# Graph attention over 200,000 sorted edges: tiles gathered once, block crossings through three extra one-hot slots, and the loads of a round in four transfers

## The reference

```python
h = (x @ W).reshape(N, H, C)
alpha = leaky_relu(a_src[src] + a_dst[dst], 0.2)      # per edge and head
m = segment_max(alpha, dst)
e = exp(alpha - m[dst])
denom = segment_sum(e, dst)
out = segment_sum((e / denom[dst])[:, :, None] * h[src], dst)
```

## Time and profile before

| what | value |
|---|---|
| median of 3 runs | 7430.2 us (7429.2 to 7434.15) |
| the profiled execution | 7443.6 us, its span 7441.7 us |
| PE, DVE, POOL busy | 69%, 68%, 71% of the span |
| three edge phases | about 2107, 2108 and 2286 us |
| four node phases | about 207, 181, 343 and 207 us |

### The profile page before, as it was taken

The page is one execution under the profiler, slowest core; times in us unless marked ns, Lnnn a source line. Parts: engine busy times, 40 slices in busy tenths (PEclk is TensorE's granted clock), DMA queues, the critical chain, the costliest instruction groups (busy, mean ns, idle before and its releaser), DMA issues. The chain is left out here.

```text
span 7441.7 us, 104504 instructions
## 1 busy us (share of the span) xinstructions
PE 5099.7 (69%) x22377; PEld 3596.7 (48%) x22378; DVE 5094.2 (68%) x15120; ACT 1891.8 (25%) x3056; POOL 5272.6 (71%) x5626
## 2 busy tenths in 40 slices
PE   7577777777777677777777776867667667676660
PEld 5354554555445445554555444554445445444440
DVE  4666666666667766666666666976666666666669
ACT  4222222222223422222222221222222222222214
POOL 1677777777774677777777775867777677777657
PEclk8677777777777877777777777987777777877775
DMA  8444444444444544444444443555444444444434
GB/s 180 128 139 137 137 137 139 138 137 136 138 138 114 163 137 137 136 139 138 137 136 138 138 137 105 172 161 140 131 136 131 134 133 132 134 132 135 129 95 133
DMA packets 559563, 1017.17 MB, mean 137 GB/s; under 512 B 203404, under 2 KB 356705, under 8 KB 558884
## 3 DMA queue, kind: packets, MB, share of 16 engines
q0 software_dynamic: 242256, 675.99, 33.8%
q1 hardware_dynamic: 246114, 270.22, 12.5%
q10 hardware_dynamic: 70514, 65.01, 2.8%
HBM read 941.47 MB, written 69.28 MB: 136 GB/s over the span
## 5 line engine op out<-in xcount | busy, mean ns | idle before, releaser
L908 POOL DMA_INDIRECT e_rows<-table,e_idx x4992 | 4770.3, 956 | 1724.0 <-issue 1434.4
L979 PE MATMUL e_p_mm<-e_rows,e_onehot 128*128 128x264 f32 x9984 | 3242.9, 480 | 390.0 <-DVE e_rows L1073 388.1
L979 PEld LDWEIGHTS e_p_mm<-e_rows,e_onehot 128*128 128x128 f32 x9984 | 2232.5, 235 | 1013.4 <-issue 590.0
L1073 DVE TENSOR_TENSOR e_rows<-e_rows,e_p_e 128x1024 f32<-128x1024 f32 x1248 | 1504.8, 1206 | 0.0
L942 ACT ACTIVATE e_onehotT<-e_onehotT,minus_pidx 128x2048 bf16<-128x2048 bf16 x312 | 624.5, 2002 | 1506.3 <-DMA e_passb<-pass_rows 1506.3
L1065 DVE TENSOR_TENSOR e_onehot<-e_col,e_p_iota 128x512 f32<-128x512 bf16 x1248 | 836.2, 670 | 108.7 <-issue 105.9
L1126 DVE TENSOR_TENSOR e_srcm<-e_p_one,e_mask 64x128 f32<-64x128 f32 (+1 forms) x312 | 89.2, 286 | 1174.5 <-PE e_p_one L1007 951.3
L975 PE MATMUL e_p_mm<-zeros 1*128 1x264 bf16 x1248 | 322.3, 408 | 643.6 <-DVE e_rows L1073 643.6
L958 ACT ACTIVATE e_rows<-e_gap 128x64 f32<-128x64 f32 (+1 forms) x312 | 85.5, 274 | 2562.3 <-DVE e_gap L1196 2562.3
L945 ACT ACTIVATE e_onehotT<-e_onehotT,one_col 128x2048 bf16<-128x2048 bf16 x312 | 624.6, 2002 | 10.3
L1164 DVE SCALAR_TENSOR_TENSOR e_top<-e_mask,e_p_small,e_seg 64x128 f32<-64x128 bf16 (+1 forms) x312 | 110.3, 353 | 742.7 <-PE e_p_small L1025 742.7
(11 more groups left out here) (214 smaller groups left out, 5536.0 us busy)
## 6 DMA issues: line engine op xcount, KB each, us to landing
e_onehotT<-rel_rows SPq DMA_DIRECT2D x312, 512.0 KB
e_rows<-table,e_idx POOLq DMA_INDIRECT x4992
table<-n_row ACTq DMA_DIRECT2D x196, 130.0 KB, 2.9
n_looprow<-table SPq DMA_DIRECT2D x196, 128.0 KB, 2.4
e_mask<-mask_rows SPq DMA_DIRECT2D x208, 80.0 KB
e_mask<-mask_rows SPq DMA_DIRECT2D x104, 160.0 KB
table<-n_row ACTq DMA_DIRECT2D x98, 132.0 KB, 1.8
n_node<-in_x_pad SPq DMA_DIRECT2D x98, 128.0 KB, 3.6
```

The lines of the kernel that those rows point to most:

```text
L908: pool.indirect_dma_start(rows[k][:, g, 0:TW], None, table[L], bass.IndirectOffsetOnAxis(ap=idx[k][:, g:g + 1], axis=0)).then_inc(s_gat[k] ...
L979: ins = nc.tensor.matmul(p_mm[:, bass.ds(region, MW)], onehot[:, g, :], rows[k][:, g, :], start=False, stop=True, skip_group_check=True)
L1073: return nc.vector.tensor_tensor(feats, feats, p_e[:, g4, :].unsqueeze(3).to_broadcast([P, 4, H, C]), ALU.mult)
```

## The change

A tile is gathered once. `TILES` is rounded up to 1568, so a layer has 98 windows. A tile belongs to the block of its first edge. Where a tile of the window reaches into a next block, one of three extra slots (`EXTRAS`) holds a second one-hot of it, relative to that block; the slots are worked through in every window, needed or not. DVE makes their one-hots and copies of the tile's messages at the start of the body (`extras`), PE multiplies them after the zeros (`extras`) and looks up three more scores into a zeroed `p_look`. Edges outside of a slot's block match nothing, so the validity mask and its addition (`srcm`) are gone, and DVE scans straight from PSUM. Windows that span four blocks or more take a new branch (`far_blocks`, on PE and DVE) that loops over all 98 blocks; the word `slow` is gone, and PE reads a flag and the words of the slots behind the first transpose. SP issues four transfers: indices and columns as one float32 row block of 67 columns (`loaded`), `onehotT` with 19 slots instead of 16, `mask` with 4 rows instead of 5, and all passes together. ACT copies the columns out of `loaded` (51 columns) behind `srcc`, and its two passes over `onehotT` are 2432 columns wide. `ACC_W` goes from 272 to 264. The tables are made in another way (`tile_tables` for `step_tables`), without the repeated gather of edges.

```diff
-                    wait_apart(sp, st["compact"], ago(BUFS))
-                    sp.dma_start(idx[k][:], src_dram[bass.ds(w, 1), :, :].rearrange("w p g -> p (w g)")
-                                 ).then_inc(s_idx[k], 16)
+                    wait_apart(sp, st["cols"], ago(BUFS))
+                    sp.dma_start(loaded[k][:], col_dram[:, bass.ds(w * COL_W, COL_W)]).then_inc(s_idx[k], 16)
...
+                    wait(act, st["settled"], ago(BUFS))
+                    nc.scalar.copy(col[k][:], loaded[k][:, 0:AT_SRC]).then_inc(st["cols"], 1)
...
+                def extras():
+                    for e in range(EXTRAS):
+                        r = (1 + e) * BANK
+                        nc.tensor.matmul(p_mm[:, r:r + MW], onehot[:, G + e, :], xmsg[:, e, :], start=False, stop=True,
+                                         skip_group_check=True)
...
                     if not first:
-                        regions = words(pe, 0, (w - 1) * G, G)
-                        slow, = words(pe, 3, (w - 1) * WIN + REGIONS, 1)
+                        regions = words(pe, REGION_ROW, (w - 1) * G, G, (REGIONS - 1) * BANK)
...
-                    offs = words(pe, 1, w * G, G)
+                    offs = words(pe, AD_ROW, w * G, G, (BLOCKS - 1) * ADS_W)
+                    flag, *extra_ad = words(pe, WINDOW_ROW, w * WIN + W_FLAG, 1 + EXTRAS, (BLOCKS - 1) * ADS_W)
+                    slots = words(pe, WINDOW_ROW, w * WIN + W_TILE, EXTRAS, G - 1)
...
+                    nc.tensor.matmul(p_look, zeros[:, 0:P], zeros[:, 0:3 * HG], start=True, stop=False, skip_group_check=True)
                     for g in range(G):
-                        last = nc.tensor.matmul(p_look[:, g * 3 * H:(g + 1) * 3 * H], onehotT[k][:, g * P:(g + 1) * P],
-                                                ad_parts[:, bass.ds(offs[g], 3 * H)], start=True, stop=True)
+                        lookup(k, g, slice(g * 3 * H, (g + 1) * 3 * H), offs[g])
+                    far_blocks(None if first else (k - 1) % BUFS, k, flag, far_count(pe, w), past)
+                    for e in range(EXTRAS):
+                        last = lookup(k, G + e, bass.ds(slots[e] * (3 * H), 3 * H), extra_ad[e])
                     last.then_inc(st["lookup"], 1)
-                    if not first:
-                        late_products((k - 1) % BUFS, slow, past)
...
+                def extras(k, slots, done, before):
+                    wait(dve, s_mm[0], before)
+                    one_hot(G, EXTRAS, k, G, p_iota[:, 0:P])
+                    dve.wait_ge(st["expo"], done)
+                    if TOPS:
+                        dve.wait_ge(st["topread"], done)
+                    flat_rows = rows[k][:].rearrange("p g m -> p (g m)")
+                    for e, slot in enumerate(slots):
+                        feats = flat_rows[:, bass.ds(slot * MW, D)].rearrange("p (h c) -> p h c", h=H)
+                        weight = p_e_flat[:, bass.ds(slot * H, H)].unsqueeze(2).to_broadcast([P, H, C])
+                        nc.vector.tensor_tensor(xmsg[:, e, 0:D].rearrange("p (h c) -> p h c", h=H), feats, weight, ALU.mult)
+                        last = nc.vector.tensor_copy(xmsg[:, e, D:MW], flat_rows[:, bass.ds(slot * MW + D, MW - D)])
+                    last.then_inc(st["extras"], 1)
...
                     if not first:
-                        off, _, _, _, slow = words(dve, 3, (w - 1) * WIN, REGIONS + 1)
+                        off, = words(dve, WINDOW_ROW, (w - 1) * WIN, 1, (BLOCKS - 1) * ACC_W)
+                        slots = words(dve, WINDOW_ROW, (w - 1) * WIN + W_TILE, EXTRAS, G - 1)
                         if not second:
-                            offs = words(dve, 3, (w - 2) * WIN, REGIONS)
+                            offs = words(dve, WINDOW_ROW, (w - 2) * WIN, REGIONS, (BLOCKS - 1) * ACC_W)
+                    flag, = words(dve, WINDOW_ROW, w * WIN + W_FLAG, 1, 2)
...
+                    if not first:
+                        extras((k - 1) % BUFS, slots, past, ago(2))
                     dve.wait_ge(s_ld[k], turns * N_LOAD)
                     dve.wait_ge(st["srcT"], now)
-                    nc.vector.tensor_tensor(srcm[:], p_src[0:HG, 0:P], m[0:HG, 0, :], ALU.add).then_inc(st["masked"], 1)
-                    dve.wait_ge(st["masked"], now)
-                    nc.vector.tensor_tensor_scan(fwd[:], m[0:HG, 1, :], srcm[:], -BIG, ALU.add, ALU.max)
+                    nc.vector.tensor_tensor_scan(fwd[:], m[0:HG, 0, :], p_src[0:HG, 0:P], -BIG, ALU.add, ALU.max)
```

More of the change, by code:

```diff
@@ L186, in on_pool @@
-            pool.wait_ge(s_p0off, 48)
-            pool.dma_start(off_row[0:3, :], off_dram[:]).then_inc(s_p0o, 16)
-            with nc.allow_non_contiguous_dma(reason="a few words per window, once"):
-                by_group = win_dram[:].rearrange("(j w) c -> w j c", w=P // G)
-                pool.dma_start(by_group[:, :, 0:REGIONS], win_i[0:P:G, :, 0:REGIONS]).then_inc(s_p0win, 16)
-                pool.dma_start(by_group[:, :, REGIONS:WIN], win_i[G - 1:P:G, :, REGIONS:WIN]).then_inc(s_p0win, 16)
@@ L192, in on_pool @@
[L192 to L202 removed]
+            nc.gpsimd.memset(zero_row[:], 0.0)
@@ L303, in step_tables @@
-        return start, on_pool, on_dve, first_blocks, columns
+            nc.vector.tensor_single_scalar(own[:], own[:], 7, ALU.logical_shift_right)
+            nc.vector.tensor_scalar(masks4[:, :, 0, :], first, -BIG, None, ALU.mult)
+            link(nc.vector.tensor_scalar(masks4[:, :, 1, :], last, -BIG, None, ALU.mult))
+            link(nc.vector.tensor_tensor(own_f[:, 1, :], own[:, 0, :], own[:, 1, :], ALU.subtract))
+            link(nc.vector.tensor_scalar(own_f[:, 1, :], own_f[:, 1, :], float(REGIONS), -FAR, ALU.is_ge, ALU.mult))
@@ L982, in product, with lookup @@
                         ins.then_inc(s_mm[g // 4], 1)
[L984 to L992 removed]
+                def lookup(k, slot, column, ad):
+                    return nc.tensor.matmul(p_look[:, column], onehotT[k][:, slot * P:(slot + 1) * P],
+                                            ad_parts[:, bass.ds(ad, 3 * H)], start=False, stop=True, skip_group_check=True)
```

563 lines of the change are left out of this document (320 added, 243 removed).

## The result

The changed kernel takes 7324.3 us (median of 4 runs, 7302.9 to 7338.8), the kernel before 7431.1 (4 runs, 7429.2 to 7434.2): ratio 0.985, 95% interval 0.982 to 0.989. On another chip it was 7314.1 against 7457.9 (0.981, 0.979 to 0.983). The forecast was slower, 7480: the sign was wrong. The time misses the forecast's own range of 7400 to 7560 and lies in the wide one, 7190 to 7690, which took in its rivals. The profiled execution took 7302.9 us, the lowest of the four.

What follows compares the result with a forecast made beforehand. POOL's gathers bound the first two edge phases, the PE-DVE ring the third; afterwards the ring everywhere. Phase terms +46 and +11, node phase -8, gave +49 on 7430.2, rounded 7480 us; own range 7400 to 7560, wide 7190 to 7690.

Steps and rivals of the forecast that it cites:

- (d): DVE's work for the extra slots: hidden in ordinary windows, +1.55 us at the loop's turn, every third window.
- half of the stall in the third phase: DVE's issue stall before L1126, third edge phase: 1.0 us per window today, 0.5 kept because moved code might keep it.
- 20.6 + 1.9: Third edge phase, us per window: ring without the stall plus the three new products, 22.5; half the stall makes 23.0.
- the gains: Savings per window on the ring: -0.31 us for srcm and its wait, -0.86 for PE's load of slow with register work.
- The ring through PE and DVE: Cycle of PE and DVE waits per window: about 19.7 us before, 21.6 mean after, above POOL's 20.15 in all phases.
- second rival: The change works as meant: ring below POOL's pace, -371 - 8, so 7051 us; chance 0.1.
- first rival: DVE's loop turn gets cheap as its body shortens: all windows ordinary at 20.8 us, third phase -116, 7194 us; chance 0.2.
- (a): Three extra-slot products on PE ahead of products(0) delay DVE's top: +1.9 us per window, bounds +1.5 and +2.9.
- gain of 1.6 for products(0): If more matmuls kept PE's full clock: products(0) 1.6 us shorter per window, with the three new products at +1.5.
- (b): PE's added register words, zero matmul and three lookups, mostly hidden in its wait ahead of the zeros: +0.25 us, bounds 0 and 0.6.
- The first node phase: Start of the kernel, before the first edge phase: new tables ready earlier, -8 us, or 0 if they aren't.
- slow rival: Fetch of DVE's code stalls the loop's turn in all phases, extras behind it: 7730 us; chance 0.2.

Runs made afterwards that it cites:

- padded kernel: The changed kernel with 60 instructions that never run added to each skipped DVE branch: 7404.3 us against 7438.5 for the kernel before (0.995).
- moved variant: The changed kernel with the three products of extras moved from ahead of products(0) to ahead of products(2): 6955.2 us against 7438.5 for the kernel before (0.935).
- kernel with the short branch: The kernel before with DVE's skipped branch late_adds cut from 16 sums to 2: 7326.8 us against 7438.5 (0.985).

## Why the prediction was wrong, step by step

**What failed, in one sum.** 7480 was forecast and 7324 measured, 156 us less. Two steps failed. The forecast kept the fetch of DVE's code, as +1.55 at the turn in (d) and as half of the stall in the third phase, and the fetch was gone. And its sum for the third phase, 20.6 + 1.9, left the gains out. The padded kernel parts the two. With the fetch back it takes 7404, so the fetch is 80 of the 156, and with it the kernel is still faster than the one before (7438 on that chip): the fetch alone does not make the sign. The other 76 is what the third phase was put too high in any case: 22.22 us per window with the fetch, where the forecast had 23.0, is 98 x 0.78 = 76. The rest, some 10 to 20 us in all, nearly cancels.

**The bound: right.** The ring through PE and DVE became the bound in the first two phases: the moved variant, with the same work in another order, brings 369 us, 1.26 per window, and ends at POOL's pace. What the change was worth without that ring was 7051 in the second rival; it is 6955, as the third phase lost its stall too.

**The turn (d): the first step that failed.** "Two more loads and 1.8 us of extras bring the scan to about 21.9" took over the 2.9 us at DVE's branch although the same text names, in its first rival, why they would go: the skipped branch shrinks from 16 copies to a loop. The runs show it from both sides, 633 packets to 76 by shortening and 82 to 604 by lengthening code that never runs. Without the fetch, (d) costs 0, measured. What is left of the turn, 22.1 to 22.2 us against 21.1 to 21.4 (medians), lies on PE: L1057's matmul takes 0.37 us there instead of 0.27 and products(0) 3.58 instead of 2.73, so PE is at the half clock sooner and longer. Why it falls sooner there is open. The forecast kept a cost whose cause the diff removes, and gave the case 0.2.

The Trainium skill (Runtime: NRT & Kernel Launch, "Instruction fetch mechanics") gives most engines room for 512 instructions in two blocks, PE for 2048, and says that a branch to outside must fetch. By that count DVE's loop of 503 would just fit if it began at a block's edge, and one of 329 in most places. The runs agree as far as they go: DVE's loops of 503 and 509 instructions were fetched at each turn, those of 329 and 251 were not. PE's loop in the changed kernel has 503 with each matmul counted once; 294 of these are matmuls, and in the trace each has at least one weight load of its own, so it is some 800 or more. With 82 packets in the whole run it was not fetched at each turn either. Where between 329 and 503 the edge lies for DVE was not tried, and no run tells a loop's length from its place.

**The third phase: the second step that failed.** 20.6 for the ring without the stall was right (20.46 in the kernel with the short branch). But "20.6 + 1.9 = 22.5" adds the new products and leaves out the gains of -0.31 and -0.86 and the cost of the words, which the sum of the ordinary window has; with them it is 21.7, measured 21.59. The first rival had it right, with 20.6 + 1.1. And the forecast kept half of a stall that went whole. The left-out terms make 98 x 0.8, some 80 us, and the half stall 49; with a little more they are the 98 x (23.0 - 21.59) = 138 us by which the phase was put too high, most of the 156. The padded kernel's 22.22 is 21.7 and the half stall, which is partly luck, as the terms below are off by more.

**The products (a): right.** +1.9 forecast; from the zeros to the top +1.58 in the ordinary window and +2.43 at the turn; three more cost 1.82. The products(0) behind them take 2.73 us (3.58 at the turn) where they took 3.89, as the clock comes back while they run. The stretches of the three products and of products(0) in the ordinary window, where the granted clock stands third from last, 0.50 and 0.71:

```profile
3033.20:3035.90 2.70, 2.70 (x7) 2.19 (x7) 0.77 (x3) 0.09 (x1) 2.09 (x3) 0.50 0.36 99
3036.00:3038.70 2.70, 2.70 (x10) 1.95 (x8) 0.00 (x0) 0.00 (x0) 1.56 (x2) 0.71 0.44 109
```

The Trainium skill (TensorE: Matmul & The Clock Gate, "HAM oscillation — how this bites in real kernels") has it that idle gaps of PE bring the half clock. The trace agrees: PE stands 3 us before L1057, and the half clock follows. What the prediction drew from it for its rival, that more matmuls would keep the full clock, didn't come: three products take 3.01 us. (Its gain of 1.6 for products(0) should have been 3.89 - 2.04 = 1.85 by its own rows.)

**Words and lookups (b): too small.** +0.25 was forecast, from 1.8 us of work against 2.08 us of PE's wait. The work is more: of the 2.08 us nothing is left, and the zeros come 0.84 us later, so it is about 2.9 us. The two word loads are 0.50 + 0.79 and 1.6 with what lies between them, where 1.0 had been taken after a short load of 0.30; the three lookups take 0.94 with their wait (0.39 and 0.55 in the timeline), where 0.6 had been taken. Without the slots' load and the lookups' register work the kernel is 0.97 per window faster. The bound of 0.6 missed it too.

**The gains: right in kind, a quarter too large.** -1.17 forecast, 9.29 to 8.44 = -0.85 measured. With the others the ordinary window is 19.72 + 0.84 + 1.58 - 0.85 = 21.3, and 21.1 to 21.4 is what the trace has; forecast 20.8. So (b), too small, and the turn, too large, nearly cancel in the mean: 21.6 against 21.23 and 21.53. A mean that fits is no proof of its terms.

**The first node phase: right in kind, too small.** -8 forecast. The first gather starts at 187.1 us instead of 209.6, and at 192.6 to 196.9 in the seven other changed kernels on normal chips (213.8 in the kernel with the short branch): some 20 us. Half of it is the node blocks' own pace, which the forecast had at nothing: the last product starts at 180 instead of 191 us, and POOL's last table transfer goes out at 109 instead of 191. That is read, not tested.

**The rivals.** The cheap turn is what happened, and its -116 in the third phase is near the -127.8; its 20.8 per window in the others had too little for the words, hence 7324 and not 7194. The slow rival had the right mechanism, DVE's code, with the opposite sign.

## What to carry to other kernels

An instruction that never runs can have a price, where it makes an engine's loop so long that its code is fetched at each turn: look at the instruction queue's packets in the profile, and count the loop's instructions before and after an edit, the skipped branches too. Before a small work is put ahead of something, ask what waits behind it: the same three products cost 1.26 us per window, and more if POOL weren't next, ahead of the signal that DVE waits for, and nothing that could be seen one wait later. Words that PE's sequencer reads hold back the matmuls behind them: without one load of 0.79 us they came 0.96 sooner, and the window was 0.97 shorter. And where two parts of a forecast price the same phase, as forecast and rival did here with 22.5 and 21.7, compare their sums.

## What was not expected of the hardware

Register loads: on PE 16 words took 1.11 us (`offs`), four words 0.50 and three 0.79; on DVE four words took 0.35, three 0.75 and one 0.31. Both loads of three read the slots' words. So the time doesn't go by the number of words; what it goes by is open.

Chips differ. On three of the five chips of the experiments the kernel before took 10018 to 10136 us instead of 7431 to 7458. The instructions themselves take as long (a gather 946 ns in the median in the kernel with the short branch, as against 947), but SP's transfers go out microseconds apart, and PE and DVE stand with "issue" or "remote" as the reason (DVE before L1126 344.5 us for "remote" between 2550 and 4400 us, none in the kernel before on the normal chip). SP's queue in the kernel with the short branch there:

```profile
3125.43 0.02 SPq L927 DMA_DIRECT2D e_mask<-mask_rows  x1
3128.56 0.00 SPq L932 DMA_DIRECT2D e_passf<-pass_rows  x1
3132.34 0.70 SPq L932 DMA_DIRECT2D e_passn<-pass_rows  x1
3137.55 0.70 SPq L932 DMA_DIRECT2D e_passb<-pass_rows  x1
```

What makes a chip slow is open. There the moved variant took 9391 us against 10136 and the padded one 10315 (1.017, 1.014 to 1.019). The changed kernel itself wasn't run there; the one without DVE's extras, which costs the same as it on a normal chip, took 10227.5 against 10131.7 (1.009, 1.006 to 1.011). So on such a chip the change is probably a small loss; that is inferred, not measured.
